# Three PSUM banks and four product buffers for the convolutions of a two-layer block on one Trainium2 core

## The reference

```python
def _L0_xattn_ref(k, v, q, ssm_kernel, D, head_dim):      # k = v = ctx, q = layernorm(x)
    kv = jnp.einsum('bhil,bhjl->bijhl', k_, v_)           # 16 heads of 8 rows, L = 256
    y = irfft(rfft(kv, 2 * L) * rfft(ssm_kernel, 2 * L))[..., :L]
    out = y + kv * D[None, None, None, :, None]
    out = jnp.einsum('bijhl,bhil->bjhl', out, q_)
x = x + tanh(g_xattn[0]) * _L0_xattn_ref(ctx, ctx, layernorm(x), L0_ssm_kernel, L0_D, 8)
x = x + tanh(g_ffn[0]) * _L0_ffn_ref(layernorm(x), ...)   # router, top 8 of 64, 8 groups: gate, up, down
x = x + tanh(g_xattn[1]) * _L1_xattn_ref(layernorm(x), ctx, mask)   # softmax attention to ctx
x = x + tanh(g_ffn[1]) * _L1_ffn_ref(layernorm(x), w_fc, w_proj)    # ternary weights, squared ReLU
```

## Time and profile before

| | before |
|---|---|
| median of 3 runs (lowest, highest) | 263.65 us (262.89, 264.14) |
| the profiled execution | 263.31 us, span 261.6 us |
| TensorE matmul busy | 232.4 us (89% of the span) |
| VectorE busy | 184.8 us (71%) |
| ScalarE busy | 109.7 us (42%) |
| GpSimd busy | 82.8 us (32%) |
| mean granted TensorE clock | 0.959 |
| first and last convolution start | 12.9 us, 90.9 us |
| first chunk starts | 81.16 us |

### The profile page before, as it was taken

How to read it: one execution, slowest core, us unless ns; L and a number is a source line. 1 busy time by engine, 2 the same in 40 slices (tenths; PEclk the granted TensorE clock), 3 DMA queues, 4 the chain that set the end, 5 groups by cost and what they waited for, 6 DMA issues and landing times.

```text
span 261.6 us, 4679 instructions
## 1 busy us (share of the span) xinstructions
PE 232.4 (89%) x1606; PEld 221.0 (84%) x1606; DVE 184.8 (71%) x514; ACT 109.7 (42%) x222; POOL 82.8 (32%) x125
## 2 busy tenths in 40 slices
PE   6395979878689999999999989999999999999973
PEld 6384978777578998998989889999899999998972
DVE  1447999998986889777999385563584753786663
ACT  0501335652103346273727655453542572363241
POOL 3559698257699530100073200100020100111110
PEclk9859899999959999999999999999999999999996
DMA  5599247000000005000000000000001001000100
GB/s 164 131 355 261 88 137 222 3 1 0 4 0 0 0 3 200 3 1 0 3 0 3 0 0 4 0 4 0 0 3 40 3 0 40 4 0 0 43 21 20
DMA packets 14038, 11.50 MB, mean 44 GB/s; under 512 B 2912, under 2 KB 13760, under 8 KB 14016
## 3 DMA queue, kind: packets, MB, share of 16 engines
q1 hardware_dynamic: 13920, 11.16, 14.1%
q10 hardware_dynamic: 96, 0.05, 0.2%
HBM read 10.14 MB, written 1.07 MB: 43 GB/s over the span
## 4 chain that ended last, share of the span: by engine, by line
PE 53%; DVE 19%; POOL 10%; issue 8%; DMA 4%; ACT 4%; DVEq 0%; POOLq 0%; ACTq 0%
PE bank L691 18%; PE bank L541 11%; PE bank L548 6%; PE bank L760 4%; POOL fold L1307 4%; POOL kv L1296 3%; PE bank L746 3%; PE bank L694 3%; DVE prod L1021 2%; POOL fold L1310 2%; DMA x_res<-in_x 2%; DMA toe<-lag_rows 2%; PE bank L732 2%; DVE act L1188 2%; PE bank L592 2%
## 5 line engine op out<-in xcount | busy, mean ns | idle before, releaser
L691 PE MATMUL bank<-w_split,xt 128*128 128x352 f32 x384 | 68.8, 328 | 0.0
L691 PEld LDWEIGHTS bank<-w_split,xt 128*128 128x128 f32 x384 | 61.3, 188 | 0.3 <-issue 0.2
L1270 POOL TENSOR_SCALAR ve<-mv 128x2 f32<-128x2 f32 (+2 forms) x16 | 3.6, 226 | 141.1 <-DVE mv L978 141.1
L1188 DVE SCALAR_TENSOR_TENSOR act<-silu,scal,bank 128x176 f32<-128x176 f32 x64 | 22.5, 393 | 17.4 <-ACT silu L883 16.6
L541 PE MATMUL bank<-d_split,a_t 128*128 128x256 f32 x264 | 33.7, 285 | 0.0
L541 PEld LDWEIGHTS bank<-d_split,a_t 128*128 128x128 f32 x264 | 32.2, 191 | 0.3 <-DVE a_t L938 0.2
L1307 POOL TENSOR_TENSOR fold<-prod 128x256 f32<-128x256 f32 x32 | 25.2, 787 | 12.2 <-DVE prod L1025 11.9
L883 ACT ACTIVATE silu<-bank 128x352 f32<-128x352 f32 x32 | 14.9, 465 | 29.2 <-PE bank L694 29.1
L592 PE MATMUL bank<-kv,toe 128*128 128x160 f32 x64 | 17.7, 363 | 10.0 <-POOL kv L1296 4.5
L592 PEld LDWEIGHTS bank<-kv,toe 128*128 128x128 f32 x64 | 11.9, 225 | 12.4 <-issue 7.5
L769 ACT ACTIVATE a_t<-bank 128x384 fp32r<-128x384 f32 (+1 forms) x32 | 14.7, 460 | 17.8 <-PE bank L548 17.7
(11 more groups left out here) (140 smaller groups left out, 437.1 us busy)
## 6 DMA issues: line engine op xcount, KB each, us to landing
toe<-lag_rows SPq DMA_DIRECT2D x4, 512.0 KB, 5.9
ring<-in_down_p SPq DMA_DIRECT2D x2, 704.0 KB, 5.1
x_res<-in_x SPq DMA_DIRECT2D x2, 512.0 KB, 4.8
ctx<-in_ctx_rows SPq DMA_DIRECT2D x2, 512.0 KB, 5.2
ring<-in_gate_p SPq DMA_DIRECT2D x2, 512.0 KB, 8.7
ring<-in_up_p SPq DMA_DIRECT2D x2, 512.0 KB, 4.1
out_x<-x_res SPq DMA_DIRECT2D x3, 256.0 KB, 2.2
tern_w<-in_w_fc SPq DMA_DIRECT2D x1, 640.0 KB, 4.3
```

Source lines behind the costliest of these rows:

```text
L691: pe.matmul(psum((name, b, c))[:, 0:CW], lhs, w_split[:, w, kt, part, cols], start=i == 0, stop=False)
L1188: drain(dve.scalar_tensor_tensor(out=act[:, g * NI:(g + 1) * NI], in0=silu[:, n % 2, cols], scalar=scal[:, b, g:g + 1], in1=psum(("up", b, ...
```

## The change

Ahead of the first chunk the convolutions take three banks in turn (Y0, Y1, DN) instead of two; behind it Y0 and Y1 by turns, by the running number of the convolution. The buffer prod gets four parts instead of two. A product hn now waits for hn - 3 folds, which is fold hn - 4. The part is chosen by the running number over both halves, in the product and in the fold. The memset at the start clears the whole buffer, 2816 elements a partition instead of 1408. TIMES, and with it every engine's order, stays.

```diff
+NPROD = 4
@@ def plan_psum
         if kind == "conv":
-            use(step, [Y0, Y1][conv % 2], 2)
+            use(step, ([Y0, Y1, DN] if i < first_chunk else [Y0, Y1])[conv % (3 if i < first_chunk else 2)], 2)
             conv += 1
@@ def build
-    prod = sb("prod", [P, 2, 2 * Q, HD, ROW])
+    prod = sb("prod", [P, NPROD, 2 * Q, HD, ROW])
@@ vector, "conv"
                     hn = half * HEADS + h
-                    if hn >= 2:
-                        dve.wait_ge(folded, hn - 1)
+                    if hn >= NPROD:
+                        dve.wait_ge(folded, hn - NPROD + 1)
                     else:
                         dve.wait_ge(prod_cleared, 1)
                     wait_filled(dve, step)
                     y = psum(step)
                     qb = h * 2 * Q * EXT
-                    o = prod[:, h % 2]
+                    o = prod[:, hn % NPROD]
...
-                    shifted_rows = view(prod, ((h % 2) * 2 * Q * HD + TAPS) * ROW + 1, [[HD * ROW, 2 * Q], [ROW + 1, 3], [1, HD]])
+                    shifted_rows = view(prod, ((hn % NPROD) * 2 * Q * HD + TAPS) * ROW + 1, [[HD * ROW, 2 * Q], [ROW + 1, 3], [1, HD]])
@@ gpsimd, "fold"
-                    p4 = prod[:, h % 2]
+                    p4 = prod[:, (half * HEADS + h) % NPROD]
```

## The result

| | before | after |
|---|---|---|
| median (lowest, highest), 14 runs each | 262.52 us (261.23, 264.14) | 261.03 us (258.97, 262.27) |
| ratio to before, 95% interval | | 0.9947 (0.9923 to 0.9972) |
| the profiled execution | 263.31 us, span 261.6 | 260.70 us, span 259.0 |
| product 4, product 16, first chunk start | 21.13, 59.92, 81.16 us | 19.39, 57.65, 78.01 us |
| product 4 to product 16 | 38.79 us | 38.26 us |

The change makes the kernel faster by 0.53% (0.28 to 0.77), which is 1.4 us; the two medians stand 1.5 us apart.

The account below looks back on a forecast made before the run. The start of the first chunk, held back by VectorE and GpSimd, was taken to set the time, with TensorE full behind it. Terms summed to 1.08 us, from the median 263.65 to 262.6 us; range 261.3 to 264.1.

Parts of the forecast that it names:

- What bounds the kernel: VectorE is full from 21 to 60 us, TensorE from 100; how much earlier chunk (0, 0) starts decides, the rest moves along.
- the prediction's own signs of being wrong: L1134 ending with fold 20, 0.50 clock after the first chunk, longer kv or folds, chunk-to-end distance changed over 0.5 us.
- The memset: Clearing the doubled tile at the start takes 2.54 us instead of 1.27, hidden by GpSimd's idle time: 0 us.
- Product 4: Its 1.21 us wait on fold 2 goes, but its convolution ends together with the fold: 0.05 us gained.
- Products up to 16: Only product 13's wait for fold 11 counts, 0.24 us gained; VectorE has no gap from product 4 to 40 us.
- Product 18: Starts 0.94 us earlier with three banks and four buffers; gather (1, 0) then waits for fold 17, 0.34 us left.
- L1134: Router's product with the reciprocal: comes 0.34 us earlier, goes before fold 20 and gains 0.35 us more.
- The rival with the most weight after the forecast: Early gains eaten: fold 20 goes ahead of L1134, only 0.4 us gained, 263.3 us; chance 0.22.
- Conv 27: Last bank wait before the first chunk; in the third bank it starts some 0.1 us sooner, gain 0.10.
- The sum: 0.05 + 0.24 + 0.34 + 0.35 + 0.10 = 1.08 us; chances faster 0.26, same 0.65, slower 0.09.
- The slower rival: A half-clock stretch reaching into the chunks costs TensorE 3.3 us, less the 1.1 gained: 265.9 us; chance 0.10.
- The better clock: Half clock from 71.9 to 78.5 us goes or shrinks: 0.4 us more, 262.1; chance 0.18 with other small gains.

Follow-up runs that it names:

- the early waits put back: The kernel after, with products 2 to 15 waiting for folds as with two buffers; 38.78 us from product 4 to 16 against 38.26, one execution, no ratio.
- the kv tile moved: The kernel after, with gather (1, 0) behind products 19 and 20 and kv (1, 4) ahead of fold 21; 0.9911 to before, again 0.9934.
- after with fillers: The kernel after, with five in place of one pair of filler matmuls ahead of the last unit's transpose; 0.9924 to before.

## Why the prediction came out as it did

**What bounds the kernel: right in the main.** The time to the first chunk counted, and what lies behind it moved along: up to about 150 us every instruction that I compared stands 3.1 to 3.2 us sooner in after than in before, as the chunk does (3.15). Behind it 0.54 us were lost, most of it at two places: about 0.2 at a few matmuls around 160 us, and 0.36 in the last ten, 2.50 us in place of 2.14. The granted clock of the last slice is 5 in after and 6 in the earlier trace rows; the larger tile with two banks has 5 too, and four buffers with two banks 6. So two of the prediction's own signs of being wrong came, a granted clock of 0.50 behind the chunk and a distance to the end changed by more than 0.5 us. The chunk itself came at 78.01 and not at 80.0 to 80.2, for the earlier start that is taken up below.

**The memset: right** in that it costs nothing: it took 2.44 us, within GpSimd's idle time, and the larger tile alone makes 1.0003. GpSimd's busy time went up by 0.9 us and not by 1.3.

**Product 4: right.** The longest of the waits was worth nothing; the equal 18.87 and 18.88 us of two and four buffers show it.

**Products up to 16: the first term that was too small.** I counted 0.24 us, and 0.52 came. There were two waits, not one. Product 9 was held 0.20 us by fold 7, which ended 0.04 us ahead of it; the gap that this left on VectorE was 0.06 us, so the list put no wait there, and I had taken "no gap up to 40 us" from the busy time. In before, fold 7 and product 9:

```profile
32.77 0.42 POOL L1310 TENSOR_TENSOR fold<-fold,prod 128x72 f32<-128x72 f32 x1
...
33.23 0.49 DVE L1021 TENSOR_TENSOR prod<-bank,q_ext 128x320 f32<-128x320 f32 x1
```

The instruction of VectorE before it had ended at 33.16. And product 13 was worth 0.32, its 0.24 of wait and the gap of some 0.08 that goes with it, since two instructions of VectorE otherwise overlap at their ends. The run with the early waits put back gave 38.78 us against 38.26, all of it. This is the term of the sum that was too small: product 9's wait stood in it at nothing.

**Product 18: right in each number.** 0.94 us earlier, 0.37 left at the gather (0.34 forecast), a new wait of 0.50 (some 0.5). But I had tied it to the third bank as much as to the buffers, and the bank has next to no part in it: 0.13 us, which the gather swallows.

**L1134: right,** and the step with the most doubt in it. 0.36 gained (0.35), by the order that one row at L953 had shown. The rival with the most weight after the forecast, that fold 20 goes first, fell with it; three runs moved the instruction against the fold, and each time it did what a lock would make it do.

**Conv 27: the wrong owner.** 0.16 us came for 0.10, and not from the bank. In all 17 traces the chunk starts 0.35 or 0.36 us behind the end of soft_t, so it waited for soft_t and not for conv 27. From the end of L1174 (L1175 of after) to the chunk it is 1.70 or 1.71 us in 16 traces, with two banks as with three, and 1.89 in before alone. There the four transposes between L1174 and soft_t took 0.85 us at a granted clock of 0.54 (79.3 to 79.8 us), and 0.66 elsewhere.

**The sum**: 1.41 us by the steps in the profile, 1.08 forecast, 1.4 by the ratio of the times. The missing third of a microsecond is the early part. It put the result just past the bound of 0.5%, where I had 0.26 and not 0.65, though the interval (0.28 to 0.77%) holds the bound. That the steps and the ratio agree so well is in part luck: the profiled pair also differs by 1.7 us at the start and 0.5 at the end, and the interval is 1.3 us wide.

**The level was the step that failed.** The gain was undersized by 0.4 us, but what put the time outside the range was the value that it was taken from. "From the median I forecast 262.6" took the median of three runs, 263.65, for the kernel's. Fourteen runs have 262.52, 1.1 us less, which is most of the 1.6 us by which the forecast missed; the other 0.4 is the gain. In other company the kernel before had medians from 262.5 to 263.4 with runs from 259.8 to 264.8 (and one of 269.8). A forecast of 261.4 from that level would have stood within 0.4 us of 261.03. The range took its width from the three runs too, 0.7 us a side, where one kernel's runs lie 3 us apart and more.

**Why they lie so far apart.** Two causes are in the traces, neither of them of this change. At the start x arrived 0.85 us sooner in after (VectorE's statistics at 4.68 in place of 5.53), toe 1.2 us sooner against the start, and convs 0 to 2 ran at full clock (0.43 us a pair) where before had them at half (0.74). Product 0 came 2.1 us sooner by it, and product 4 1.7, as conv 4 in its turn ran at half clock in after. The run with two buffers and the larger tile had the early start as well. And half-clock stretches fall in different places from trace to trace: around convs 23 to 26, in the last unit, twice near 150 us, once on the first chunk.

**The slower rival** had the right mechanism and the right price (at most 3.3 us for a full slice forecast, 1.3 to 2.2 measured against the usual 180.6) and, as far as the times show, the wrong owner: such a stretch came behind the chunk with two banks and two buffers too, and the third bank alone made 1.0000. The rule on cycling through PSUM banks that the prediction cites from the Trainium skill (TensorE: Matmul & The Clock Gate, section A second HAM failure mode: psum-queue depth-cycling) finds no support in that. It isn't refuted: one of three traces with two banks had a stretch, and seven of fourteen with three.

**The better clock** was undersized. With full clock from within conv 24 on the way from L1135's end to the chunk is 11.56 us, with half clock 12.45 to 12.49: 0.9 us, not 0.4. I had priced the one wait that the trace showed, at product 24. It is worth 0.3 (L1175 starts 9.42 us behind L1135's end in place of 9.75). The other 0.6 is in L1175 itself, another product of VectorE with its inputs in SBUF. The first fence is of after, the second of the early waits put back:

```profile
75.26 0.77 POOL L1308 TENSOR_TENSOR fold<-prod 128x256 f32<-128x256 f32 x1
75.28 1.03 DVE L1175 TENSOR_TENSOR soft_parts<-rt,soft_parts 128x256 fp32r<-128x256 f32 x1
```

```profile
75.59 0.43 DVE L1175 TENSOR_TENSOR soft_parts<-rt,soft_parts 128x256 fp32r<-128x256 f32 x1
75.89 0.78 POOL L1308 TENSOR_TENSOR fold<-prod 128x256 f32<-128x256 f32 x1
```

It took 1.03 or 1.04 us in the eight traces where the fold's step began just ahead of it, and 0.42 or 0.43 in the five where it came 0.2 to 0.3 us before the step; in the four with the kv tile moved it took 0.87. So the step that I had read at L1134 stands once more on the way to the chunk, in before too, and I had not looked for it. The clock doesn't decide it alone: in after with fillers product 24 waited 0.38 us, and L1175 still went first. No run moves L1175 by itself.

Open remains what decides where a half-clock stretch falls, and with it why a version that is at the chunk 1.5 us sooner shows 1.0 us of it in one company and none in another.

## What to carry to other kernels

A wait in the list is worth only the distance to what would have ended next: of four product waits the longest (1.21 us) was worth nothing, the second (0.86) 0.37 directly, and one whose gap was too short to be listed 0.20. Ask of each buffer how many are in use at the worst place before adding one: three did as well as four, and the bank, added for the same purpose, did nothing by itself. When a step moves by tenths of a microsecond, look at what it then meets on the other engine's port, there and at each later instruction of the kind up to the landmark. Where a time comes out of one trace and a stretch at half clock can fall anywhere, compare distances up to the stretch. And take the level of a forecast from more than three runs.

## What the runs showed of the hardware

- VectorE's product of two tensors in SBUF (128 by 128, f32) takes 0.29 us alone, 0.36 to 0.39 when it begins 0.53 to 0.55 us into a fold's step of 0.77 us on GpSimd, 0.63 to 0.65 at 0.3 us into it, and 0.80 at 0.1 us. Each time it ends 0.14 us behind the step. Where it begins in the small step before, it goes ahead of the GpSimd instruction that is next in the queue, and that one then takes 0.83 to 0.86 us. The product of 128 by 256 at L1175 takes 0.43 ahead of the step and 1.03 just behind its start. Products of 320 elements that read PSUM are not held (0.45 to 0.49 us in every trace).
- Adding 0.2 us of work ahead of the first of these products moved its end by 0.7 us, adding 0.8 by 0.8.
- In four of the 15 traces without fillers the granted clock fell to 0.50 on the last hidden products, 4.36 us for 20 matmuls in place of 2.35, and in a fifth somewhat earlier. TensorE had been idle for 1.2 us shortly before in all 15, so this gap alone doesn't decide it.
